# A gated delta-rule attention block with a spline-weight FFN on one NeuronCore: the order of the block solve, of the spline cubics and of the first load of x

## The reference

```python
xn = _layernorm(x, axis=-1)
x = x + _L0_attn_ref(xn, ...) + _L0_ffn_ref(xn, ...)
# attention: 6 heads, keys of 64, values of 128
q, k, v = short_conv(xn @ Wq), short_conv(xn @ Wk), short_conv(xn @ Wv)   # 4 taps, then silu
beta, g = sigmoid(xn @ Wb), -exp(A_log) * softplus(xn @ Wa + dt_bias)
o = gated_delta_rule(q, k, v, g, beta)       # S = S e^g; S += k (v - k S) beta; o = q S
o = rmsnorm(o) * norm_weight * silu(xn @ Wg);  attention = o @ Wo
# FFN: three dense weights are Catmull-Rom interpolations of control points
ffn = (silu(xn @ gate_w.T) * (xn @ up_w.T)) @ down_w.T
```

## Time and profile before

| what | us |
|---|---|
| median of 3 runs | 853.06 |
| the three runs | 851.47, 853.06, 857.05 |
| the profiled execution | 857.5 |
| its span, first to last instruction | 855.8 |
| PE busy in the span | 777.6 |
| DVE busy | 579.8 |
| ACT busy | 469.9 |
| POOL busy | 382.2 |

### The profile page before, as it was taken

How to read it: one execution, slowest core, us unless ns; L and a number is a source line. 1 busy time by engine, 2 the same in 40 slices (tenths; PEclk the granted TensorE clock), 3 DMA queues, 4 the chain that set the end, 5 groups by cost and what they waited for, 6 DMA issues and landing times.

```text
span 855.8 us, 15467 instructions
## 1 busy us (share of the span) xinstructions
PE 777.6 (91%) x5688; PEld 451.9 (53%) x5688; DVE 579.8 (68%) x1401; ACT 469.9 (55%) x1078; POOL 382.2 (45%) x415
## 2 busy tenths in 40 slices
PE   2989689998978999997999997898789999999998
PEld 1465366746547766645774654765234444444443
DVE  4899977778866868895788797567864435444400
ACT  3757836643784764686665487567753333333200
POOL 4386986577692655686454768013330000000000
PEclk9989789998989999899999999999999999999999
DMA  7330031330021022003023001056772422312111
GB/s 228 110 87 16 10 98 50 103 77 23 13 74 48 28 96 84 1 0 121 11 89 96 15 1 35 6 205 157 168 201 62 127 68 65 87 56 67 38 50 37
DMA packets 59937, 62.21 MB, mean 73 GB/s; under 512 B 30391, under 2 KB 45100, under 8 KB 59862
## 3 DMA queue, kind: packets, MB, share of 16 engines
q1 hardware_dynamic: 53526, 44.97, 18.6%
q0 software_dynamic: 4224, 13.11, 5.1%
q10 hardware_dynamic: 2112, 3.15, 1.1%
HBM read 33.69 MB, written 19.73 MB: 62 GB/s over the span
## 4 chain that ended last, share of the span: by engine, by line
PE 63%; DVE 16%; POOL 10%; issue 5%; ACT 3%; DMA 3%; SPq 0%; POOLq 0%; DVEq 0%; ACTq 0%
PE bank L663 16%; PE pd L1996 7%; PE pd L1997 7%; PE pd L1998 6%; DVE cv L1060 3%; PE bank L749 2%; PE bank L823 2%; PE bank L740 2%; PE bank L875 2%; POOL cv L1657 2%; POOL rn L1638 1%; PE bank L851 1%; PE pg L1982 1%; PE bank L807 1%; PE pg L1983 1%
## 5 line engine op out<-in xcount | busy, mean ns | idle before, releaser
L663 PE MATMUL bank<-x_parts,w 128*128 128x512 f16 x576 | 130.6, 385 | 1.5 <-DVE x_parts L1017 1.5
L2066 DVE TENSOR_TENSOR hh<-sg,pu 128x512 f32<-128x512 f32 x64 | 43.9, 686 | 93.9 <-ACT sg L2035 92.7
L1948 POOL DMA_DIRECT2D yr<-y_attn x16 | 8.8, 554 | 191.8 <-DMA out<-yr 191.7
L663 PEld LDWEIGHTS bank<-x_parts,w 128*128 128x128 f16 x576 | 56.4, 99 | 70.0 <-issue 7.4
L663 PE MATMUL bank<-w,x_parts 128*128 128x384 f16 x384 | 79.1, 365 | 8.1 <-ACT V L1432 7.9
L2035 ACT ACTIVATE sg<-pg 128x512 f32<-128x512 f32 x64 | 38.0, 594 | 64.3 <-PE pg L1983 64.3
L663 PEld LDWEIGHTS bank<-w,x_parts 128*128 128x128 f16 x384 | 39.9, 109 | 40.7 <-issue 12.0
L1060 DVE SCALAR_TENSOR_TENSOR cv<-raw,taps,cv 128x512 f32<-128x512 f32 x72 | 55.1, 830 | 0.0
L1638 POOL TENSOR_TENSOR rn<-t,mhalf 128x6 f32<-128x6 f32 x16 | 22.8, 1423 | 68.6 <-DVE t L1229 68.6
L1996 PE MATMUL pd<-dw,it 128*128 128x512 f16 x128 | 49.0, 383 | 0.0
L1997 PE MATMUL pd<-dw,it 128*128 128x512 f16 x128 | 49.0, 383 | 0.0
(11 more groups left out here) (306 smaller groups left out, 2054.2 us busy)
## 6 DMA issues: line engine op xcount, KB each, us to landing
xb<-in_x SPq DMA_DIRECT2D x4, 1024.0 KB, 6.5
xr<-in_x SPq DMA_DIRECT2D x16, 256.0 KB, 2.6
y_attn<-xr SPq DMA_DIRECT2D x16, 256.0 KB, 2.1
down_rows<-inv SPq DMA_DIRECT2D x8, 512.0 KB, 5.5
yr<-y_attn POOLq DMA_DIRECT2D x16, 256.0 KB, 2.9
out<-yr SPq DMA_DIRECT2D x16, 256.0 KB, 2.0
xn_hi<-x_parts POOLq DMA_DIRECT2D x4, 512.0 KB
xn_lo<-x_parts POOLq DMA_DIRECT2D x4, 512.0 KB
```

Of the source, the lines that this page charges most:

```text
L663: ins = nc.tensor.matmul(out, a, b, start=first and i == 0, stop=last and i == 2)
L2066: v.tensor_tensor(hh[:, i % 2, :], sg[:, i % 2, :], pu[i % 2][:], ALU.mult).then_inc(h_ready, 1)
```

## The change

Four edits. (1) In PE's solve the X products of chunks 1 and 3 come ahead of the gate products of their turn. (2) The last V transposes (vtr 5) come at the end of turn 4 in place of its beginning; ACT reads them after the last X2, and DVE's right sides of chunk 0 wait for that. (3) DVE does all of `slopes`, `curved` and `shifted` ahead of the first inverse; the high and low parts come at turns 0 and 2. (4) x of stage 0 comes in two halves, tiles 0 and 1 by SP, tiles 2 and 3 by ACT ahead of its weight pieces, which no longer wait for x; DVE waits for the second half ahead of tile 2's statistics.

```diff
-    def spline_slopes(self, dve):
+    def spline_cubics(self, dve):
         dve.wait_ge(self.small_in, self.SMALL)
         dve.wait_ge(self.ctrl_in, 16)
         self.cubics.slopes(dve)
+        self.cubics.curved(dve)
+        self.cubics.shifted(dve)
 
     def coefficients_high(self, dve):
-        self.cubics.shifted(dve)
...
                 for k in range(NCH + 3):
                     if k in (1, 3):
+                        crossed(s, k)
                         gate_products(s, 2, k // 2)
-                    if 1 <= k < NV - 1:
+                    if 1 <= k < NV - 2:
                         v_transposes(s, k + 1)
-                    if k < NCH:
-                        ps, f = claim(("X", k), s)
...
+                    if k in (0, 2):
+                        crossed(s, k)
...
+                    if k == NV - 2:
+                        v_transposes(s, NV - 1)
...
                 for t in range(NCH):
+                    if s.first() and t == NCH // 2:
+                        dve.wait_ge(x_half, 16)
                     v.bn_stats(stats[:, t, :], xb[:, t, :]).then_inc(ln_step, 1)
...
-                    if k == 0 and s.first():
-                        prep.cubics.curved(dve)
...
+                    if k == 0 and s.first():
+                        prep.coefficients_high(dve)
                     if k == 2 and s.first():
-                        prep.coefficients_high(dve)
-                    if k == 3 and s.first():
                         prep.coefficients_low(dve)
 
             def right_sides(s, c):
 
+                if c == 0:
+                    ready(dve, ("vtr", NV - 1), s)
...
-                    v_tokens(s, c + 2)
+                    if c < NCH - 1:
+                        v_tokens(s, c + 2)
                     u = ("X2", c)
...
+                v_tokens(s, NV - 1)
...
-            prep.load_piece(act, 0)
-            act.wait_ge(x_in, 16)
-            for i in range(1, NSTG):
+            act.dma_start(xb[:, NCH // 2:, :], x_v[0][:, NCH // 2:, :]).then_inc(x_half, 16)
+            for i in range(NSTG):
                 prep.load_piece(act, i)
...
-            load_x(s0, None)
+            sp.dma_start(xb[:, 0:NCH // 2, :], x_v[0][:, 0:NCH // 2, :]).then_inc(x_in, 16)
```

More of the change, by code:

```diff
@@ L593, in attend @@
         done = [sem(f"done{i}") for i in range(8)]
+        x_half = sem("x_half")
         x_in, ln_step, ln_stats, ln_rstd, xn_ready = sem("x_in"), sem("ln_step"), sem("ln_stats"), sem("ln_rstd"), sem("xn_ready")
@@ L758, in v_transposes, with crossed @@
                 ins.then_inc(f, 1)
+            def crossed(s, k):
+                ps, f = claim(("X", k), s)
+                for h in range(NH):
+                    for even, odd in zip(EVEN, ODD):
+                        ins = nc.tensor.matmul(ps[odd, SUB * h:SUB * h + SUB], BA[even, 0, ch(k, h), odd],
+                                               Tc[even, ch(k, h), :], start=True, stop=True)
+                ins.then_inc(f, 1)
             def solve(s):
@@ L1274, in local @@
                 if s.first():
-                    prep.spline_slopes(dve)
+                    prep.spline_cubics(dve)
                 invert_blocks(s)
@@ L1776, in load_x @@
             def load_x(s, b):
-                if b is not None:
-                    sp.wait_ge(v_conv, b.val(NV, NV))
+                sp.wait_ge(v_conv, b.val(NV, NV))
                 sp.dma_start(xb[:], x_v[s.idx()]).then_inc(x_in, 16)
```

## The result

Ten runs each, medians: 857.38 us before, 847.19 after. The ratio is 0.9899, with an interval of 0.9874 to 0.9923, so 8.7 us less (6.6 to 10.8). Forecast was 0.9888. The changed kernel's profiled execution took 851.86, its span 850.1 against 855.8, and it is the slowest of its ten (the others 844.10 to 850.25, at granted clocks of 0.957 to 0.966 against its 0.955). So the two traces differ by 5.7 where the medians differ by 10; the reader must see which rows carry the change and which the clock. Every ratio in this document leaves out executions more than 1.5% above the fastest of their kernel (one of ten of the kernel "One queue for x and Wk", four of eleven of "The moments behind the right sides", none of the others).

A forecast was written before the change was run, and what follows sets the result against it. The chain lies 63% on PE, with waits in the solves, DVE's cubics crowding stage 0's, and all beginning with x. Start and stage 0 -3.7, three solves -5.9, sum -9.6: from 853.06 to 843.5 us, range 840.5 to 848.5.

The forecast's parts named there:

- the start and stage 0: From the load of x to the norm of chunk 0 in stage 0: 3.7 us less, not 5.1.
- Rival C: In the solves, the bank wait is replaced by one on ACT or DVE; only X products count: -4.9, 848.2; chance 0.14.
- B: Rival for stage 0: POOL does not bind, as its operations shorten without DVE's cubics or with earlier loads; -11.0, 842.1; chance 0.12.
- A: Rival for the start: x arrives as late as before, since both queues share the engines; sum -7.6, 845.5; chance 0.14.
- X ahead of the gate products, V transposes at the end of turn 4: Solves of stages 1 to 3: X products moved into PE's gap give 0.40; with the transposes moved, 1.97 a stage, -5.9 together.
- Latest is ACT's copy: Solve of stage 1: ACT's X2 copy is the last thing turn 5 waits for; it starts at 265.53, not 267.52.
- x in halves: Start of the kernel: x is in at about 6.0, not 8.02, so -2.0; bounds 0 and 2.5.
- Cubics ahead of the inverse: Stage 0: ten DVE operations ahead of the inverse cost 2.6 there, bounds 2.0 and 8.5, and leave the solve.
- PE is 5.1 earlier in chunk 0 of `recur`: Stage 0: first gate product of `recur` at 122.3 instead of 126.14, 3.8 earlier, plus 1.3 from the higher clock.
- POOL takes most of that over: Stage 0: POOL's 30 cubic operations, started 1.65 earlier and keeping 24.04 us, limit the gain to 3.7 instead of 5.1.
- the 1.72 of waiting ahead of the norm: Stage 0, ahead of the norm at 139.08: POOL's wait disappears, as DVE is there 5 earlier; 1.72 of the 3.7.
- Rival D, the clock: Turns 3 to 6, stages 1 to 3: PE's granted clock falls, costing 4.7 a stage; sum +4.5, 857.6; chance 0.04.

The follow-up runs named there:

- One queue for x and Wk: Changed kernel, but x as one transfer first on SP's queue with Wk behind it, other weight pieces on ACT's queue; ratio 0.9939 to before.
- The moments behind the right sides: Changed kernel, with DVE's seven layer norm moments behind the right sides of chunk 1, chunk 0's norm ahead of the layer norm's power on POOL; ratio 0.9985 to before.
- the last kernel: Kernel with earlier gate product and later fifth V copies, plus keys and state products ahead of the solve's last turn, right sides ahead of last Z2 copy; 835.21 us, 0.9743.

## Why the prediction was right or wrong

*The size.* The ratio came right: 0.9888 against 0.9899, well within the interval. In part that is luck, for the working behind it did not hold in every term. In the two traces the start and stage 0 give 2.55 of the 3.7 forecast, the three solves 5.2 of 5.9, and a lower clock takes 3.4 back in two other places. Only one execution of after was profiled, the slowest of its ten, so what the terms gave in the others is not shown. The absolute 843.5 was 3.7 low: it was reckoned down from 853.06, the median of before's first three runs, and ten gave 857.38, 4.3 more. Rival C (0.9943) is outside the interval, B (0.9872) just outside, A (0.9911) inside by its number, but its reason is not: x did come earlier. B's premise, that POOL does not bind, held in after's trace, but hardly for B's reasons: POOL's cubics took 23.67 in place of 24.04.

*X ahead of the gate products, V transposes at the end of turn 4.* The mechanism is right, the size nearly: 1.97 a stage forecast, 1.81, 1.74 and 1.68 measured. (From the first gate product to that of `recur` stages 2 and 3 take 17.9 in place of 19.6; stage 1, with a part at 1.2 GHz, 19.3 in place of 20.7, where 18.7 was forecast.) "Latest is ACT's copy" held: 0.49, 1.03 and 0.49 of ACT stand on the chain. Turn 5 came 15.51 behind the first gate product, forecast 15.34: ACT's copy ended where I had it, but its hand-over to PE takes 0.25 (the "issue" at 262.65), and I had counted 0.03. DVE's new wait cost nothing.

*x in halves.* Undersized: the statistics came 2.37 earlier, not 2.0, near the bound of the ramp. The rule of the Trainium skill (DMA: Bandwidth & Descriptors, Rules for kernel authors) and the trace do not differ: no bandwidth was gained (238 GB/s in the first 8 us, 233 before), and with Wq beside it x was back at 7.91. The gain in x's arrival is in the order of bytes.

*Cubics ahead of the inverse: the step that failed.* First, the cost "I take 2.6" was 3.65 (71.35 to 75.00): nine at 0.28 or 0.29 and the last at 1.34, with waits between. The prediction had POOL waiting in that gap, but from 73.58 POOL ran an operation of 1.27 (L1663), and the last of the ten, issued 0.08 behind it with two SBUF inputs, took 1.34; alone they take 0.28. That is about the 1.05 that was missing. Second, "PE is 5.1 earlier in chunk 0 of `recur`" was 2.9: the gate product of `recur` came at 123.23, not 122.3, and at 3.32 and not 2.06, since I took stage 1's clock for stage 0. That this clock follows from the change is not shown: in the kernel with POOL's cubics cut PE has the same list and ran the product in 2.12. Third, "POOL takes most of that over": its cubics did start 1.77 earlier (the silu ahead of their loads only 0.97 earlier, not 1.65, so the agreement is luck) and end at 133.85 (134.3 forecast), but they bound nothing; DVE's chain of state, moments, outputs and squares ended last, 1.4 longer by POOL beside it. That the 1.72 of waiting ahead of the norm goes failed with it. DVE's state update 2.96 earlier (130.14 for 133.10), less 0.41 that the moments took longer than before (2.71 for 2.30), is the 2.55. The step was near its edge, though: with the solve's order alone and in the last kernel POOL does bind, rn (137.81 and 135.42) directly behind `rstd`. The rule on shared SBUF interfaces (the Trainium skill, GPSIMD Engine Reference, Key points) would have told more than I took from it: of the moments, three of the five with two SBUF inputs ran at 0.57 to 0.62 beside POOL and 0.16 or 0.17 without, `tensor_scalar` at 0.17 in both.

*Rival D, the clock.* Had 4 in 100 as a full loss, and came as a small one: 1.6 in one of three stages, in the profiled run. That the change "takes idle time out of these turns and adds none" was no argument for the clock. Nor is the loss shown to be the change's: the kernels with the solve's order alone and without the third edit have the same order of products there and kept 1.00 in that place.

## What to carry to other kernels

Price work that starts earlier at the clock that it will find, not at that of its old place: 3.8 us of earlier start in stage 0 were given back whole, 1.9 of them by one product at half the clock. An engine whose last operation stands directly ahead of the joint need not bind it: cut its work and see whether it then waits, as POOL did. Look for large products that stand behind a wait for a bank; moving one to a place where PE idles anyway, and small products into the gaps between turns, took another 13 us beyond the change's 8.7 (by the ratios 0.9743 and 0.9899).

## What the runs showed of the hardware that was not expected

PE's granted clock rose and fell within one solve: 0.82, 0.50 and 0.83 in three windows of 4 us from 106 in the kernel with the curved part in the gap, after PE had been busy 3.82 of 4 us with small products; in the changed kernel it stood at 1.00 from 110 to 122 after 4.00 of 4, then at 0.57 from 122 to 126, though PE had not idled for more than 0.65 us at a time since 104. Before had 4.08 of 6 us busy from 262 and kept 1.00; after had 4.86 of 6 in the same stretch and got 0.80, and the kernel without the third edit had 4.86, too, and kept 1.00. So these rows give no simple rule, and the same list of products can get either clock. The same products took 2.12, 3.28 or 4.02 us by it.

Runs of one kernel spread over 8 us (844.10 to 851.86), near what the whole change is worth. Beside POOL, three of DVE's operations of 128x4 took 0.57 to 0.62 us in place of 0.16 or 0.17, nearly fourfold, though these move almost nothing.
